# Second-half scores moved out of the hidden-layer bank, and the ramp orders of four engines rewritten

## The reference, cut to what matters

```python
# x: (32 sequences, 128 steps, 128 channels), cond: (32, 128); 16 heads of 8, 8 experts
x = x + attn(cond_attention(x, cond))      # "stage 1" and the linear attention below
x = x + moe(recurrence(x, cond))           # 128 dependent steps, then top-2 of 8 experts

def cond_attention(query, target, ...):    # stage 1
    q = (query @ Wq + bq), sharded into 16 heads of 8
    scores = softmax(q @ k / sqrt(8))      # 16 x 16 per token: own head against 16 heads of the target
    context = scores @ v
    return context @ Wo + bo
def attn(x, ...):                          # linear attention over heads
    q = softmax(q); k = elu(k) + 1
    context = cumsum(k (x) v, heads) / (cumsum(k, heads) + EPS)
    return (q . context) @ Wo + bo
def recurrence(x, h0, ...):
    for each of the 128 steps:
        hid, out = sigmoid([x_t, h] @ W + b)
        h = out * h + (1 - out) * tanh(x_t @ Wx + bx + hid * (h @ Wh + bh))
```

## Time and profile before

| | us |
|---|---|
| median of 3 runs | 370.85 |
| lowest, highest | 369.77, 373.18 |
| the profiled execution | 373.52 |
| its span, first to last instruction | 371.8 |
| of it: up to the second half of stage 1 | 0 to 37.7 |
| of it: second half of stage 1 and first tile's way to the recurrence | 37.7 to 72.2 |
| of it: first tiles | 72.2 to 86.2 |
| of it: the rest of the tiles and the end | 86.2 to 371.8 |

### The profile page before, as it was taken

The page is one execution under the profiler, slowest core; times in us unless marked ns, Lnnn a source line. Parts: engine busy times, 40 slices in busy tenths (PEclk is TensorE's granted clock), DMA queues, the critical chain, the costliest instruction groups (busy, mean ns, idle before and its releaser), DMA issues.

```text
span 371.8 us, 9072 instructions
## 1 busy us (share of the span) xinstructions
PE 360.4 (97%) x2514; PEld 303.6 (82%) x2514; DVE 318.1 (86%) x1163; ACT 294.4 (79%) x1141; POOL 262.8 (71%) x279
## 2 busy tenths in 40 slices
PE   6999998999999999999999999999999999999996
PEld 5588887777888888888888888888888888888875
DVE  3366899599999999999999999999999999998541
ACT  2455675458999999998989999999998999987764
POOL 4599354398778777877787778778777877777200
PEclk9999997899999999999999999999999999999999
DMA  7500000000000000000000000000000000000000
GB/s 223 217 2 0 4 0 3 0 2 2 9 8 10 8 9 8 10 9 9 10 8 10 7 11 8 12 12 8 10 8 10 8 11 7 10 10 7 10 9 14
DMA packets 7442, 6.76 MB, mean 18 GB/s; under 512 B 736, under 2 KB 6112, under 8 KB 7392
## 3 DMA queue, kind: packets, MB, share of 16 engines
q1 hardware_dynamic: 6816, 5.84, 4.9%
q10 hardware_dynamic: 576, 0.35, 0.4%
HBM read 4.09 MB, written 2.10 MB: 17 GB/s over the span
## 4 chain that ended last, share of the span: by engine, by line
PE 79%; DVE 13%; issue 3%; DMA 1%; ACT 1%; ACTq 0%; DVEq 0%
PE bank L406 69%; PE bank L564 7%; DVE kvs L1168 3%; DVE att L1177 2%; PE bank L452 2%; DVE mem L1219 2%; DMA XT<-in_x_t_dram 1%; DVE h L1239 1%; DVE rden L1160 1%; DVE bank L1231 1%; DVE bank L1224 1%; PE bank L516 1%; PE bank L508 1%; DVE bank L1128 0%; DVE CTX L1096 0%
## 5 line engine op out<-in xcount | busy, mean ns | idle before, releaser
L361 POOL TENSOR_TENSOR qc<-kvs,qn 128x512 f32<-128x512 f32 x64 | 81.5, 1273 | 50.8 <-DVE kvs L1168 50.0
L406 PEld LDWEIGHTS bank<-h,gwh 128*128 128x128 f32 x512 | 67.8, 191 | 18.7 <-DVE h L1239 14.9
L349 POOL TENSOR_TENSOR kv<-kv,qkv 128x512 f32<-128x512 f32 x64 | 80.0, 1272 | 0.2
L1168 DVE TENSOR_TENSOR_SCAN kvs<-bank,kv 128x256 f32<-128x256 f32 x128 | 79.7, 664 | 0.2 <-issue 0.2
L895 ACT ACTIVATE hid<-bank,gw 128x128 f32<-128x128 f32 x253 | 75.8, 371 | 2.8
L406 PE MATMUL bank<-rw,h 128*128 128x392 f32 (+2 forms) x192 | 74.7, 471 | 0.1
L406 PE MATMUL bank<-h,gwh 128*128 128x32 f32 x512 | 72.2, 264 | 1.8 <-DVE h L1239 1.8
L406 PE MATMUL bank<-w,hsq 128*128 128x128 f32 x512 | 64.3, 279 | 0.0
L406 PEld LDWEIGHTS bank<-w,hsq 128*128 128x128 f32 x512 | 59.9, 192 | 0.1
L406 PE MATMUL bank<-h,whw 128*128 128x64 f32 x256 | 53.0, 289 | 0.0
L924 ACT ACTIVATE gt<-bank 128x64 f32<-128x64 f32 x128 | 29.8, 233 | 25.5 <-PE bank L406 24.2
(11 more groups left out here) (118 smaller groups left out, 715.6 us busy)
## 6 DMA issues: line engine op xcount, KB each, us to landing
out_dram<-res SPq DMA_DIRECT2D x32, 64.0 KB
XT<-in_x_t_dram SPq DMA_DIRECT2D x7, 256.0 KB, 5.8
rw<-in_rw_dram SPq DMA_DIRECT2D x1, 516.0 KB, 5.7
w<-in_w_dram SPq DMA_DIRECT2D x1, 512.0 KB, 6.5
XT<-in_x_t_dram ACTq DMA_DIRECT2D x1, 256.0 KB, 5.6
aw<-in_aw_dram SPq DMA_DIRECT2D x1, 192.0 KB, 4.4
gwx<-in_gw_dram SPq DMA_DIRECT2D x1, 128.0 KB, 5.0
gwh<-in_gw_dram SPq DMA_DIRECT2D x1, 128.0 KB, 4.7
```

The lines of the kernel that those rows point to most:

```text
L349: pool.tensor_tensor(kv[:, a * D:b * D, :].rearrange("p (d e) h -> p d e h", d=D // 2), kv[:, D * D + a:D * D + b, :].unsqueeze(2).broadca ...
L361: pool.tensor_tensor(qc[:, a:b, :, :], kvs[:, a * D:b * D, :].rearrange("p (d e) h -> p d e h", d=D // 2), qn[:, p, a:b, :].unsqueeze(2).b ...
L406: return pe.matmul(dst, w, rhs, start=start, stop=True, skip_group_check=True)
L1168: dve.tensor_tensor_scan(flat(kvs[:, a:b, :]), scan_mask, flat(kv[:, a:b, :]), 0.0, ALU.mult, ALU.add).then_inc(kv_sum, 1)
```

## The change

Three things are edited. The scores of units 13, 14 and 15 move from the banks HID, OUT and HID to OUT, Z and OUT, with the waits that this needs: `scores(14)` waits for the reader of unit 11 in Z, `scores(15)` for that of unit 13 in OUT, `gates_bias(0)` and `x1_bias(0)` for the last scores of Z and OUT; `hidden(0)` no longer waits for scores in HID. The ramps of TensorE, ScalarE, VectorE and GpSimd are written in another order. One of the unread matmuls moves from behind `project_out(0)` to in front of `context(13)`; their number stays. The order of two or three instructions changes in the finales of ScalarE and VectorE too. No operation is added or removed.

```diff
-            return (MEM, Z, MEM, Z, MEM, HID, OUT, HID)[u - QUADS]
+            return (MEM, Z, MEM, Z, MEM, OUT, Z, OUT)[u - QUADS]
...
-                at_least(pe, s_sub, u - 1 if u not in (13, 14) else 0)
+                at_least(pe, s_sub, 0 if u == 13 else 12 if u == 14 else u - 1)
...
-                    pe.wait_ge(s_sub, 2 * QUADS)
...
                 att_T(0)
+                fill(1, HID[:, 2 * P:])
                 context(13)
                 probs_T(15)
                 context(14)
                 fill(1, HID[:, 2 * P:])
                 context(15)
                 project_out(0)
-                fill(3, HID[:, 2 * P:])
+                fill(2, HID[:, 2 * P:])
                 qkv_of(2)
...
-                    act.wait_ge(s_sub, 12)
+                    act.wait_ge(s_sub, 15)
...
-                    act.wait_ge(s_sub, 15)
+                    act.wait_ge(s_sub, 2 * QUADS)
...
             def finale():
+                x_rows_out(30)
                 square(30, 0)
-                x_rows_out(30)
```

More of the change, by code:

```diff
@@ L373, in ramp @@
                 outer(0, 0, 0)
+                outer(0, 0, 1)
                 queries(0, 0)
                 weigh(0, 0, 0)
-                outer(0, 0, 1)
                 weigh(0, 0, 1)
@@ L594, in ramp @@
                 qkv_of(0)
+                scores(10)
+                scores(11)
                 probs_T(8)
-                scores(10)
+                scores(12)
+                probs_T(9)
                 context(8)
-                probs_T(9)
-                scores(11)
-                scores(12)
+                scores(13)
                 probs_T(10)
-                scores(13)
-                scores(14)
                 context(9)
                 probs_T(11)
+                qkv_of(1)
+                scores(14)
                 context(10)
-                qkv_of(1)
+                probs_T(12)
+                scores(15)
                 context(11)
-                scores(15)
-                probs_T(12)
                 probs_T(13)
@@ L933, in ramp @@
                 qkv_bias(0)
+                qkv_out(0, 0)
                 exps(8)
-                qkv_out(0, 0)
+                qkv_bias(1)
+                exp_qk(0, 0)
                 probs_out(8)
                 exps(9)
-                exp_qk(0, 0)
+                exps(10)
+                exps(11)
                 probs_out(9)
-                exps(10)
-                qkv_bias(1)
                 context_raw(8)
                 probs_out(10)
-                gates_bias(0)
-                exps(11)
+                exps(12)
+                memory_bias(0)
                 context_raw(9)
                 probs_out(11)
+                exps(13)
                 context_raw(10)
                 qkv_out(1, 1)
-                exps(12)
+                probs_out(12)
                 context_raw(11)
-                exps(13)
-                probs_out(12)
                 exps(14)
                 probs_out(13)
+                context_raw(12)
+                exp_qk(1, 1)
                 x1_bias(0)
[L957 to L960, removed]
                 att_out(0)
                 exps(15)
+                probs_out(14)
                 context_raw(13)
                 probs_out(15)
-                qkv_bias(2)
                 context_raw(14)
                 context_raw(15)
+                qkv_bias(2)
+                gates_bias(0)
                 x1_out(0, 0)
@@ L1248, in ramp @@
                 less_largest(10)
+                largest(11)
                 query_sum(0, 0)
                 key_sums(0)
+                less_largest(11)
                 divisors(0)
-                largest(11)
+                largest(12)
                 inverses(0, 0)
-                less_largest(11)
                 inverses(0, 1)
                 sum_heads(0, 0)
+                less_largest(12)
+                largest(13)
                 sum_heads(0, 1)
[L1258 to L1261, removed]
                 less_largest(13)
+                inverse_sum(8)
                 sum_heads(0, 2)
                 sum_heads(0, 3)
+                largest(14)
+                normalise(8)
                 less_largest(14)
+                largest(15)
                 head_max(1, 1)
-                largest(15)
                 less_largest(15)
+                less_max(1, 1)
                 add_dims(0, 0)
                 add_dims(0, 1)
-                less_max(1, 1)
-                inverse_sum(8)
-                normalise(8)
                 inverse_sum(9)
+                inverse_sum(10)
                 normalise(9)
-                inverse_sum(10)
                 inverse_sum(11)
@@ L1280, in ramp @@
                 normalise(11)
+                sum_heads(1, 0)
                 normalise(12)
+                key_sums(1)
                 inverse_sum(13)
-                sum_heads(1, 0)
+                sum_heads(1, 1)
+                query_sum(1, 1)
+                inverse_sum(14)
+                divisors(1)
                 normalise(13)
-                sum_heads(1, 1)
+                normalise(14)
+                inverse_sum(15)
+                normalise(15)
                 sum_heads(1, 2)
-                inverse_sum(14)
-                key_sums(1)
-                normalise(14)
+                inverses(1, 0)
                 sum_heads(1, 3)
[L1291 to L1296, removed]
                 head_max(2, 0)
                 less_max(2, 0)
+                inverses(1, 1)
                 query_sum(2, 0)
@@ L1365, in finale @@
                 less_top(31)
+                taken_inverse(31, 1)
                 relu(31, 1, 0, 2)
                 relu(31, 1, 1, 0)
-                taken_inverse(31, 1)
             pipeline(dve, ramp, iteration, finale)
```

## The result

| | before | after |
|---|---|---|
| median of 20 runs each, us | 370.64 | 368.15 |
| lowest, highest | 367.83, 373.18 | 366.83, 369.1 |
| ratio of the runs, 95% interval | | 0.9928 (0.991 to 0.9946) |
| profiled execution, its span | 373.52, 371.8 | 369.1, 367.3 |

The change makes the kernel 0.7% faster: 2.5 us by the medians, 2.0 to 3.3 us by the interval. The spread of the runs has shrunk by more than the median fell, from 5.4 to 2.3 us: the highest run came down by 4.1 us, the lowest by 1.0.

The account below looks back on a forecast made before the run. TensorE, busy 97% of the span, bounds the kernel; only the ramp can win, where VectorE is the engine to count. Terms 0 + 1.3 + 2.0 + 0 = 3.3 us off the median 370.85 gave 367.5 us, range 365.9 to 370.5.

Parts of the forecast that it names:

- Part one: Ramp up to the first attention output and context(13): no gain, within 0.7 us either way; add_dims(0) ends at 58.0.
- (a): Rival: the clock falls all the same, or the median before had less fall; 370.0 or 368.8 us; chance 0.32.
- (c): Rival: idle spell at 57 us brings the fall sooner, half clock until the recurrence; 372.5 us; chance 0.05.
- Part two, the order: From context(13) to qkv_of(2): earlier exp_qk(1) and outer(1), less VectorE work behind them; gain 1.3 us.
- Part two, the clock: Same stretch, up to qkv_of(2): the clock's fall costs 2.0 us, won if the clock holds.
- I take the 3.3 off the median: Whole gain from the profiled execution (373.52 us) subtracted from the median of 370.85, giving 367.5 us.
- Part three: From qkv_of(2) to memory(0), VectorE's first of the recurrence: same work, stays at 4.47 us.
- the finale: Swapped instructions at the kernel's end: the next TensorE step waits for both in each case, so nothing.
- The sum: Gains of the ramp's stretches and the kernel's end: 0 + 1.3 + 2.0 + 0 = 3.3 us.
- (b): Rival: normalise(8) finds GpSimd idle and later ones pass between its instructions; 366.1 us; chance 0.11.
- The milestones: Signs of being right in the ramp: qkv_of(2) at 64 to 65 us, memory(0) at 68.5 to 69.5.

Follow-up runs that it names:

- e6: Changed kernel with second-half contexts in two banks, context(13) ahead of att_T(0), ScalarE reordered, VectorE's normalise moved behind work not waiting for GpSimd: 367.39 us.
- e1: Kernel before, with only one of three unread matmuls moved from behind project_out(0) to in front of context(13): 370.58 us, ratio 0.9972.
- e7: Changed kernel with less_max(1) put back behind add_dims(0), as it was before: 369.03 us, ratio 0.9939 to before.
- e8: Changed kernel with GpSimd's outer(0,0,1) put back behind weigh(0,0,0): 374.37 us, ratio 1.0084 to before.
- e2: Changed kernel with the one moved unread matmul put back behind project_out(0), the order alone: 369.53 us, ratio 0.9979 to before.
- e10: Changed kernel without the four unread matmuls ahead of qkv_of(2): 370.94 us, ratio 0.9995 to before.
- e9: Changed kernel with GpSimd's old order as in e8, plus four unread matmuls, two behind context(12) and two behind probs_T(14): 370.7 us, ratio 0.9978.
- e3: Changed kernel with the scores of units 13 to 15 back in the old banks with the old waits: 368.45 us, ratio 0.9936 to before.

## Why the prediction was right, and where it wasn't

**The time.** 367.5 us was forecast, and a range of 365.9 to 370.5; 368.15 was measured. Within 1% of no change had the largest chance, and it was so.

**Part one, up to `context(13)`: a gain of 0, measured 0.66 us** (17.57 to 16.91 after `qkv_of(0)`), within the 0.7 that was allowed. The stall of `normalise(8)` is there: 0.94 us instead of 0.15, where 0.7 more were predicted. What the Trainium skill says in "SBUF — State Buffer", section "SBUF: two separate sides", the traces confirm: `normalise(8)` ends at 53.25, `weigh(0)` at 53.16, and with GpSimd idle six `normalise` take 0.70 us (e6). The step that was too large is the sum of VectorE's busy time. `add_dims(0)` was put at 58.0 us, 16.5 after `qkv_of(0)`, and ended at 56.51 us, 15.9 after it. From `head_max(0)` on it took 14.2 us and not 14.85. The three new instructions took the 1.3 us that they were put at, so the 27 old ones took 12.9 us, where the prediction carried over their 13.55 us busy from the trace before. Probably an instruction overlaps its neighbour only when nothing is waited for (`largest` takes 0.68 us, and the next one in a full queue starts 0.60 behind it), and VectorE waited several times in that stretch before and never now; no run tests this. The idle spell of TensorE ahead of `att_T(0)`, on which rivals (a) and (c) counted with 1.2 us, was 0.47 us, mostly for the same reason.

**Part two, the order: 1.3 us, measured 1.21.** (`normalise(10)` and `normalise(11)` were the blocked ones, not 9 and 10.) Between `context(13)` and `qkv_of(2)` lie 6.78 us in e1 (old order, clock held) and 5.57 in the changed kernel; 5.5 had been predicted. GpSimd's `outer(1)` ends 1.3 us earlier, where 1.1 were predicted. That `exp_qk(1)` behind an earlier `less_max(1)` is the reason, as the prediction put it, holds for 0.6 of it (e7). GpSimd's own earlier `outer(0)` the prediction had only as an idle time of VectorE in part one, 1.06 us. Taken out of the new lists it costs 1.9 us at `att_T(0)` (e8). That is its price in the new lists and not its share of the gain: no run gives the old lists this one edit.

**Part two, the clock: 2.0 us, measured 1.95 between the traces, but only some 0.5 between the medians.** For a run with the fall of the trace the term is right: 8.73 us from `context(13)` to `qkv_of(2)` before, 6.78 in e1. The step that failed is "I take the 3.3 off the median". The profiled execution had a whole fall; of 71 runs of that kernel 28 had none, and six a short one that shows no cost. How far the median lies above that of the held runs depends on the share that falls: 0.3, 0.7 and 1.5 us in the three sessions (370.77, 370.75 and 371.42 against 370.52, 370.08 and 369.95). The 20 runs of the result have 370.64, and their clocks are not recorded. The sentence behind the sum, that less is to be won if the median run hadn't the whole fall, and rival (a) had this, with the spread of 3.4 us as the sign. What the Trainium skill says in "TensorE: Matmul & The Clock Gate", section "Part 1: The HAM clock gate (the "warmup" mystery)", that the same kernel is caught differently from run to run, agrees with 43 falls in 71 runs. What that page says of transposes in "Part 4: PE-mode transpose" no run here shows.

**Part three and the finale: nothing, measured 0.06 us more and nothing.** From `qkv_of(2)` to `memory(0)` it takes 4.53 us against 4.47, and the rest of the span is the same to 0.1 us.

**The sum.** In the traces: 0.66 + 1.21 + 1.95 - 0.06 = 3.76 us, forecast 3.3. In the medians: about 2.0 for the order (370.1 to 368.15, held runs), and the 0.5 that is left of the 2.5 for the clock, an estimate. So the order, forecast at 1.3, was worth more and the clock, forecast at 2.0, less, and the two errors partly cancelled: that the time came out near isn't all merit.

**The rivals.** (a) was half true: the clock doesn't fall any more, but the median before had less of it. That the new order alone holds it is refuted (e2, six of twelve fell). (b) isn't so, the stalls are all there. (c), the early fall that outlasts the stage, doesn't occur in this kernel. e8 comes nearest, at 374.4 us and with 1.9 us more of waiting: its profiled fall begins before `att_T(0)`, but it is over by `context(15)`, which takes 1.01 us at 64.15. How far the longer falls of its other runs reach isn't recorded.

**The milestones.** `qkv_of(2)` at 63.1 and `memory(0)` at 67.6 us lie ahead of the 64 to 65 and 68.5 to 69.5 that were named; 0.85 us of both is the earlier start.

**Open.** No trace shows why a fall is short in one run and long in another, or absent, and where else the moved matmul would do was not tried. That a short fall shows no cost before because TensorE waits 1.3 us for VectorE in that stretch (e1) is argued, not shown; that e10 pays 1.4 us for one behind that wait agrees with it.

## What to carry to other kernels

When a kernel's profile shows a short stretch at the lower clock, look at the clocks of many runs before the stretch goes into a sum: the profile is one draw, and the median gets only the share of runs that fall. If TensorE idles by turns ahead of such a stretch, try one or two matmuls that nobody reads in the idle spell: here one held the clock there at no cost (e1), and the same matmul behind the spell didn't (the kernel before, e2). And compare traces from a milestone in front of the edit, not from zero: the start-up of a kernel moved by more than this whole change.

## What was not expected of the hardware

With one unread matmul of 256 columns (0.5 us) moved into an idle spell the clock stayed up in twelve of twelve runs (e1: all at 1.000); with it behind the spell 43 of 71 fell. Taking four away made it fall in eleven of twelve (e10), and adding four to an order that fell in seven of seven (e8) held it in twelve of twelve (e9).

The start of the kernel, up to `qkv_of(0)`, varies between 39.3 and 41.9 us. The landing of the first transfer of x is a part of it: 5.05 us in the trace after, 5.58 in the trace before and 5.94 in that of e3. The matmuls right behind it are another part, 6.99, 7.32 and 7.40 us in these three traces. The other end varies hardly: from `memory(0)` to the end of the span it takes 299.6 to 299.9 us in all thirteen profiled executions, so between these only the start and the ramp make the difference. That the start is also most of the spread of 2 to 3 us among the held runs of one kernel is likely, but each kernel was profiled once; e3's profiled execution has the latest start (41.90) and is its slowest run (370.41, median 368.45).
